# Rotary queries with the dimensions on the partitions, in a decoder layer on one Trainium2 core

## The reference, cut to what matters

```
q = rmsnorm(x @ w_qa, q_norm_w) @ w_qb            # per head: q_nope (128), q_rope (64)
rotate_half(x) = concatenate([-x[..., 32:], x[..., :32]])
q_rope = q_rope * cos + rotate_half(q_rope) * sin
k_rope = k_rope * cos + rotate_half(k_rope) * sin  # one for all heads
scores = (q_nope . k_nope + q_rope . k_rope) / sqrt(192)
```

## Time and profile before

| | |
|---|---|
| median of 3 runs | 1356.03 us (1355.33 to 1356.2) |
| the profiled execution | 1356.68 us, span 1354.9 us |
| busy: PE | 1039.2 us, 77% of the span, 7438 instructions |
| busy: weight loads (PEld) | 632.5 us, 47% |
| busy: DVE | 1088.9 us, 80%, 2984 instructions |
| busy: ACT | 539.4 us, 40% |
| busy: POOL | 239.7 us, 18% |
| mean granted clock of PE | 0.90 |
| chain that ended last | PE 40%, DVE 25%, issue 23%, ACT 5%, POOL 5% |

### The profile page before, as it was taken

How to read it: one execution, slowest core, us unless ns; L and a number is a source line. 1 busy time by engine, 2 the same in 40 slices (tenths; PEclk the granted TensorE clock), 3 DMA queues, 4 the chain that set the end, 5 groups by cost and what they waited for, 6 DMA issues and landing times.

```text
span 1354.9 us, 22533 instructions
## 1 busy us (share of the span) xinstructions
PE 1039.2 (77%) x7438; PEld 632.5 (47%) x7460; DVE 1088.9 (80%) x2984; ACT 539.4 (40%) x1225; POOL 239.7 (18%) x475
## 2 busy tenths in 40 slices
PE   1635687799999999998999999997743552547998
PEld 0423354455555555555555565564332231324554
DVE  5679587988888988988988988887179878876886
ACT  1539444434434434344444444443024321533443
POOL 1000012112112112112112121211022313131111
PEclk9659889999999999999999999999875776767999
DMA  9100022332332342322442333455361000000001
GB/s 360 55 1 0 1 53 49 73 58 57 58 56 54 65 116 53 66 55 46 70 119 47 66 61 61 94 92 147 79 218 39 24 31 0 0 0 8 39 31 47
DMA packets 199388, 86.30 MB, mean 64 GB/s; under 512 B 173560, under 2 KB 184824, under 8 KB 198784
## 3 DMA queue, kind: packets, MB, share of 16 engines
q1 hardware_dynamic: 199296, 85.12, 26.9%
HBM read 35.80 MB, written 7.34 MB: 32 GB/s over the span
## 4 chain that ended last, share of the span: by engine, by line
PE 40%; DVE 25%; issue 23%; ACT 5%; POOL 5%; DMA 1%; ACTq 0%; SPq 0%; DVEq 0%; POOLq 0%
PE bank L1765 10%; PE bank L1715 5%; DVE arena L1438 4%; PE bank L1649 4%; PE bank L1750 4%; DVE arena L1414 3%; PE bank L1681 2%; DVE arena L1431 2%; POOL arena L418 2%; PE bank L1733 2%; PE bank L1737 2%; PE bank L1735 2%; PE bank L1734 2%; PE bank L1736 2%; DVE scal L1532 1%
## 5 line engine op out<-in xcount | busy, mean ns | idle before, releaser
L1160 ACT ACTIVATE arena<-bank,arena,scal 128x128 f32<-128x128 f32 (+3 forms) x256 | 157.9, 617 | 356.6 <-POOL arena L1018 356.6
L1765 PE MATMUL bank<-arena 128*128 128x512 f16 x768 | 187.8, 391 | 7.1 <-DVE arena L1477 4.3
L1438 DVE SCALAR_TENSOR_TENSOR arena<-arena 128x128 f16<-128x128 f32 (+3 forms) x256 | 169.3, 661 | 9.1
L1414 DVE TENSOR_REDUCE arena<-bank 128x1 f32<-128x128 f32 (+3 forms) x256 | 124.2, 485 | 60.4 <-PE bank L1738 60.3
L1018 POOL TENSOR_TENSOR arena<-arena,scal 128x1 f32<-128x1 f32 x256 | 49.0, 191 | 551.2 <-DVE arena L1414 551.2
L1715 PE MATMUL bank<-arena 128*128 128x512 f16 x576 | 136.4, 382 | 0.5 <-DVE arena L1470 0.5
L1750 PE MATMUL bank<-arena 128*128 128x512 f16 (+3 forms) x768 | 116.8, 302 | 10.8 <-DMA arena<-arena 10.8
L1765 PEld LDWEIGHTS bank<-arena 128*128 128x128 f16 x768 | 73.6, 100 | 90.4 <-issue 16.5
L1431 DVE TENSOR_SCALAR arena<-arena 128x128 f16<-128x128 f32 (+3 forms) x256 | 109.9, 429 | 3.0 <-issue 0.3
L1750 PEld LDWEIGHTS bank<-arena 128*128 128x128 f16 x768 | 70.3, 99 | 50.4 <-issue 13.1
L1733 PE MATMUL bank<-arena 128*128 128x128 f16 (+3 forms) x256 | 77.3, 302 | 4.7 <-issue 3.3
(11 more groups left out here) (213 smaller groups left out, 2119.7 us busy)
## 6 DMA issues: line engine op xcount, KB each, us to landing
arena<-in_L_attn_w_qb SPq DMA_DIRECT2D x1, 4608.0 KB, 23.5
arena<-in_x SPq DMA_DIRECT2D x4, 1024.0 KB, 5.9
arena<-in_L_attn_w_o SPq DMA_DIRECT2D x1, 4096.0 KB, 33.9
arena<-arena SPq DMA_TRANSPOSE x256, 2.8
arena<-in_fside_BxS2xS SPq DMA_DIRECT2D x4, 1024.0 KB, 5.7
arena<-in_L_ffn_w SPq DMA_DIRECT2D x8, 512.0 KB, 8.3
out<-arena SPq DMA_DIRECT2D x16, 256.0 KB, 2.0
arena<-in_x SPq DMA_DIRECT2D x12, 256.0 KB, 3.0
```

What stands on the lines that cost most here:

```text
L1160: act.activation(pf(k), banks[S_BANKS[g % 3]][:, 0:n], ACT.Exp, bias=NB[:, k:k + 1], scale=sc_exp, accum_out=SUM[:, k:k + 1]).then_inc(s_e ...
L1414: dve.tensor_reduce(NEGM[:, (g & 3):(g & 3) + 1], banks[S_BANKS[g % 3]][:, 0:n], AX.X, ALU.max, negate=True).then_inc(s_max, 1)
L1438: dve.scalar_tensor_tensor(out=ph_part(k, 1), in0=pf(k).rearrange("p (t c) -> p t c", c=P), scalar=R4[:, k:k + 1], in1=ph_part(k, 0), op0= ...
L1765: last = pe.matmul(banks[Y_BANK][:, :], ot(gp, a, k, (q & 3) * P, P), wo(b, gp * GH + k), start=(k == 0 and n == 0), stop=(k == GH - 1 and ...
```

## The change

The product of the rotary queries is turned round: the weights are the stationary operand and the latents of all 512 tokens the moving one, so the bank holds 128 dimensions (two heads of 64) by 512 tokens after nine instructions. What was a stride within a partition is now a place on another partition. ACT copies the bank to RSW in four pieces of 32 partitions, each to the place of its neighbour (`rope_swap`, at the end of step 3); POOL multiplies RSW by the sine (`rope_sin`); DVE multiplies the bank by the cosine (`rotate`), now behind the splits of step 4, and waits for `rope_swap` before; POOL adds. `rope_hi` stands now in step 6, ahead of `qn_hi_`: one conversion into RHI for the low part and four of 64 partitions into QR, which put each head's rotary part on both halves of the partitions. POOL's `rope_split` writes the low part into QR. The transposes and the copies behind them are gone. The tables are wanted with dimensions on the partitions (COST, SINT): PE transposes them as float32 after the first `prep_mm`, ACT copies them out; the keys keep a table of half the width, for which there is a second load.

```diff
-        ROPE = take(2 * TB * 2 * DR)
+        ROPE = take(2 * TB * DR)
+        COST, SINT = take(L), take(L)
...
-            sp.dma_start(ROPE, rope_tab).then_inc(tab_in, 16)
+            sp.dma_start(ROPE.rearrange("p (a d) -> p a d", d=DR),
+                         rope_tab.rearrange("p (a h d) -> p a h d", h=2, d=DR)[:, :, 0, :]).then_inc(tab_in, 16)
+            sp.dma_start(ROPEF, rope_tab).then_inc(tab_in, 16)
...
+            def rope_sin(i):
+                pool.wait_ge(r_swap, i + 1)
+                pool.tensor_tensor(RSW, RSW, SINT, ALU.mult).then_inc(r_sin, 1)
             def rope_sum(i):
                 pool.wait_ge(r_rot, i + 1)
-                pool.tensor_tensor(RT1, RT1, RT2, ALU.add).then_inc(r_sum, 1)
+                pool.wait_ge(r_sin, i + 1)
+                pool.tensor_tensor(RT1, RT1, RSW, ALU.add).then_inc(r_sum, 1)
+            def rope_split(i, par):
+                pool.wait_ge(r_own, i + 1)
+                pool.tensor_tensor(QR[:, (par * 3 + 2) * L:(par * 3 + 3) * L], RT1, RHI, ALU.subtract).then_inc(r_split, 1)
...
                         if g == 4:
+                            rope_sin(i + 1)
+                        if g == 5:
                             rope_sum(i + 1)
-                        if g == 5:
-                            rope_split(i + 1)
+                        if g == 6:
+                            rope_split(i + 1, 1 - j)
...
+            def rope_swap(i):
+                act.wait_ge(r_mm, i + 1)
+                if i > 0:
+                    act.wait_ge(r_sum, i)
+                for a in range(0, P, 64):
+                    for o in (0, 32):
+                        last = act.activation(RSW[a + o:a + o + 32, :], banks[R_BANK][a + 32 - o:a + 64 - o, :], ACT.Copy)
+                last.then_inc(r_swap, 1)
+            def rope_hi(i, par):
                 act.wait_ge(r_sum, i + 1)
-                act.activation(v[:, :, 1, :], RT1.rearrange("p (a d) -> p a d", d=DR), ACT.Copy)
-                act.activation(v[:, :, 0, :], RT1.rearrange("p (a d) -> p a d", d=DR), ACT.Copy).then_inc(r_hi, 1)
+                act.activation(RHI, RT1, ACT.Copy).then_inc(r_own, 1)
+                for h in range(2):
+                    o = (par * 3 + h) * L
+                    for a in range(0, P, DR):
+                        last = act.activation(QR[a:a + DR, o:o + L], RT1[h * DR:(h + 1) * DR, :], ACT.Copy)
+                last.then_inc(r_hi, 1)
...
                     if g == 6 and not last:
+                        rope_hi(i + 1, 1 - j)
                         qn_hi_(2 * i + 2, 0)
...
-                    if g == 4 and not last:
-                        rope_hi(i + 1)
+                    if g == 3 and not last:
+                        rope_swap(i + 1)
...
             prep_te(0, T_BANK)
+            act.wait_ge(tab_t, 1)
+            act.activation(COST, banks[0][:, :], ACT.Copy).then_inc(tab_made, 1)
+            act.activation(SINT, banks[1][:, :], ACT.Copy).then_inc(tab_made, 1)
...
-                dve.tensor_tensor(RT1, q, c, ALU.mult)
-                dve.tensor_tensor(t4[:, :, 0, :], q4[:, :, 1, :], s4[:, :, 0, :], ALU.mult)
-                dve.tensor_tensor(t4[:, :, 1, :], q4[:, :, 0, :], s4[:, :, 1, :], ALU.mult).then_inc(r_rot, 1)
-            def rope_out_hi(i, par):
-            def rope_out_lo(i, par):
+                dve.wait_ge(r_swap, i + 1)
+                dve.tensor_tensor(RT1, banks[R_BANK][:, :], COST, ALU.mult).then_inc(r_rot, 1)
...
-                for t in range(TB):
-                    k = 0
-                    for c in range(QC):
-                        for a, b in TRI:
-                            last = pe.matmul(banks[R_BANK][:, t * P:(t + 1) * P], ct(bp, a, c, t * P, P),
-                                             wr(b, c, i & 7), start=(k == 0), stop=(k == 3 * QC - 1))
+                for c in range(QC):
+                    for a, b in TRI:
+                        last = pe.matmul(banks[R_BANK][:, :], wr(b, c, i & 7), ct(bp, a, c, 0, L),
+                                         start=(k == 0), stop=(k == 3 * QC - 1))
...
-                    pe.wait_ge(r_teh, i + 1)
-                    pe.wait_ge(r_tel, i + 1)
+                    pe.wait_ge(r_hi, i + 1)
+                    pe.wait_ge(r_split, i + 1)
...
-                        if g == 6:
-                            rope_t_hi(i + 1)
-                        if g == 7:
-                            rope_t_lo(i + 1)
...
             prep_mm(0)
+            rope_tables()
```

More of the change, by code:

```diff
@@ L106, in decoder_layer @@
         XA = take(TB * D)
[L107 removed]
+        RSW = take(L)
+        RHI = take(L, fp16)
         PT = take(2 * 2 * TB * L, fp16)
```

95 lines of the change are left out of this document (32 added, 63 removed).

## The result

| | before | after |
|---|---|---|
| median of six runs, same chip | 1355.8 us | 1349.04 us (1346.42 to 1350.17) |
| profiled execution, and its span | 1356.68, 1354.9 | 1346.42, 1344.6 |
| busy DVE, PE | 1088.9, 1039.2 us | 1043.2, 1016.5 us |
| busy ACT, POOL | 539.4, 239.7 us | 678.7, 273.1 us |

The ratio is 0.9937, 95% interval 0.9915 to 0.9959: 0.6% faster, where 1345.5 us (a ratio of 0.992) was forecast. I read the waits first, as before the change: us in total, times, longest, 160 to 900 us of the changed kernel.

The account below looks back on a forecast made before the run. Neither PE nor DVE is full; they hand the limit to each other through waits. Terms -7 - 5 + 3.8 - 2.3 = -10.5 us on 1356.68 gave 1346.2, median 1345.5; own range 1339 to 1352, wider range 1326 to 1364.

Parts of the forecast that it names:

- pairs 0 to 3: First four head pairs, without output products: little wait of DVE to give, so a gain of 0.
- pairs 4 to 23: Ten double pairs of the walk, each forecast at -0.7 us: together -7 us.
- M7 to M3: From a pair's step 7 row maximum on DVE to the next pair's step 3: 8.85 us odd, 13.2 even.
- M4 to M5: Row maximum of step 4 to that of step 5; in odd pairs from 3.80 to 2.37 us.
- M5 to M7: Row maximum of step 5 to that of step 7; in odd pairs up from 5.57 to 7.2 us, behind ACT's conversions.
- the hold: POOL's sum slowing DVE's 512-column split L1438 before the change, 1.64 for 0.75 us: 0.89 us lost.
- Rival 1: POOL's sine product beats DVE's split in odd pairs and those without preparation: 0.85 us in 20 pairs, 1362 us; chance 0.20.
- The clock: PE's idle time puts preparation products at the lower clock: 1.2 us in one even pair of two.
- +1.5: Ahead of the walk and first pair: tables cost +3.8 us, first pair's rotary chain gains 2.3 us.
- Rival 3: Small ACT copies cost by their partitions, so conversions shrink by 1.1 us in 24 pairs: 1319 us; chance 0.10.
- Rival 4: Walk exchanges PE's wait for ACT's queue and gains nothing: 1357.5 us; chance 0.12.
- Rival 2: Lower clock covers the preparation's products in all 12 even pairs, 2.2 us each, +26: 1371 us; chance 0.08.

Follow-up runs that it names:

- e5: Changed kernel with two full 128x512 conversions instead of four of 64 partitions (rotary scores not the reference's): 1313.56 us, ratio 0.9670.
- e12: Changed kernel with rotary tables built behind the preparation loop and ACT's five conversions split, three after copy L1183, two behind the exponentials: 1316.96 us, ratio 0.9711.
- e4: Changed kernel with the four 32-partition exchange copies replaced by one 128x512 copy, leaving the exchange out: 1356.78 us, ratio 1.0006.
- e14: Kernel with split conversions and late tables, and in even pairs DVE's cosine product put in front of the 128x512 split: 1310.5 us, ratio 0.9669.
- e1: Changed kernel with ACT's five conversions of the rotated queries issued behind the exponential of step 6: 1344.67 us, ratio 0.9920.
- e6: Kernel before the change with DVE's three rotary products moved from in front of the splits to behind them: 1388.84 us, ratio 1.0236.
- e7: Kernel before the change with PE's transposes of the rotated queries' high parts moved from its seventh step to its eighth: 1367.07 us, ratio 1.0070.
- e2: Changed kernel with the rotary tables' eight transposes and two copies moved behind the preparation loop: 1343.0 us, ratio 0.9910.

## Why the prediction was right, and where not

**The sum.** 10.5 us were forecast for the profiled execution and 10.3 measured, and that closeness is partly luck: by sections the start came out 3.5 us better than forecast, pairs 0 to 3 1.7 us and pairs 4 to 23 2.0 us worse. By the medians it is 6.8 us.

**The pairs.** Where the clock was full, every stretch was within 0.11 us of the forecast: odd M7 to M3 8.80 (8.85 forecast; pair 14 to 15), M4 to M5 2.37 (2.37), M5 to M7 7.15 (7.2); even M7 to M3 13.31 (13.2), M3 to M7 15.41 (15.5). The mechanism was the forecast one: PE's wait and the hold go, DVE's wait for L1183 comes. e5 and e12 show that it is this wait which limited the gain. That pairs 4 to 23 gave 5.0 and not 7 lies in the comparison: I took pairs 13 and 14 (51.27) for the mean of before, and ten double pairs take 511.01, 51.10 each. Forecast for after were 50.57, measured 50.6.

**ACT's small instructions.** The price of one was right, the overlap was not: the four start 0.6 us apart, 2.38 and 2.53 us for four, where I took 2.1 and 2.2. Neighbours of 128 partitions had overlapped by 0.1. Half of the 0.6 us falls in M5 to M7, which took the 7.15 us all the same, since from M5 to the first conversion (508.38 to 510.42) it was 2.0 us where I had put 2.3. POOL's sum did fall on the next split, as forecast: L1464 on 128 columns took 0.91 us from 509.56, beside L1035, and 0.29 alone.

**The port.** The sine product did not meet the split in odd pairs. Between L1471's start (507.11) and the exchange's end (507.50) lay 0.4 us, not the 0.2 I had read, and 0.9 from the start of L1464 (506.58). Rival 1 with its price is real (e4), only its condition did not occur. I named the wrong victim: in even pairs it is L1464, with one SBUF operand, and not L1471. The Trainium skill ("SBUF — State Buffer", section "Who interferes with whom") says that a DVE instruction with at most one SBUF input keeps clear of GpSimd only outside the two-port modes, and names `tensor_scalar` among the operations that can use them; the 1.48 us of e4 and the 0.95 of e14 agree.

**The clock.** Forecast: 1.2 us in every second even pair. The penalty was 1.2 us in three of ten (pairs 8, 12, 20), and 0.83 on the way from M7 to M3 of four odd pairs (5, 9, 13, 21), ahead of which products had run slowly behind a wait for a split:

```profile
487.84 4.31 PE L1765 MATMUL bank<-arena 128*128 128x512 f16 x12 [2.42 <-DVE arena L1477]
```

3 x 1.2 + 4 x 0.83 = 6.9 against 6 in the sum: the total was near, half of its places were not. PE's idle time before the preparation's transposes grew as forecast, but to 1.5 to 2.3 us (0.79 before) and not to 2.7.

**Ahead of the walk.** +1.5 was forecast, and this pair of executions reads -2.0. The chain step was near (L1158 at 40.51 against 41.2, +3.1). Then two things gave back: the fourth preparation product ran mostly at the higher clock (granted 0.81 against 0.56), 3.84 us for 5.40, so that the chain was only 1.3 us late at the 8.7-us reduction (80.60 for 79.28), and the rotary product of pair 0, for which I had put 3.8, took 2.10:

```profile
67.56 3.84 PE L1663 MATMUL bank<-arena 128*128 128x384 f16 x24
...
152.26 2.10 PE L1694 MATMUL bank<-arena 128*128 128x512 f16 x9 [1.46 <-DVE arena L1342]
```

Neither belongs to the change. e1 has the same program up to M3 of pair 0; there the fourth product took 5.38 us, and the rotary one

```profile
153.42 3.59 PE L1695 MATMUL bank<-arena 128*128 128x512 f16 x9 [1.46 <-DVE arena L1343]
```

(granted clock 0.57, in the changed kernel's execution 1.00), and M3 of pair 0 came at 177.65, not 174.99. e6 and e7, with the program of before, have it at 175.32 and 177.19 for 177.02. So the clock moves this section by 2 to 3 us from execution to execution, about as much as the forecast and the reading differ by; the -2.0 can't be credited to the change, and whether the +1.5 was right stays open. That the tables cost some 3 us up to the reduction is shown by e2 and the kernels beside it.

**Pairs 0 to 3.** Forecast 0, measured 1.7 lost. I had argued that there is little wait to give there, which was right; but DVE's new wait for L1183 came all the same: M3 to M7 took 12.16 for 11.1 in the odd pairs and 15.43 for 14.7 and 15.0 in the even ones, 3.3 us in four pairs, of which M7 to M3 gave 1.6 back.

**Rivals.** Rival 3 is out (0.587 and 0.624 us). Rival 4 is half true: PE's 32.0 us of waiting became 67.8 us of DVE's, and 5.0 us stayed in pairs 4 to 23. Rival 2 did not come: the lower clock took three of the preparation's products, not twelve.

## What to carry to other kernels

An exchange of partition groups by ACT costs a whole instruction for each group, whatever its height (32 and 64 partitions here); count the instructions. Then place them: the same work cost 27.6 us more or less, as it stood in front of something due or in the idle time between two exponentials. An operation that is moved off PE and DVE is paid where its new engine is next waited for, so ask for each place what queues behind it, and try the split of a long group before any other way round it. Before a saving of 2 or 3 us is read from one execution, look at the same stretch in another kernel with the same program there.

## What the hardware showed that I had not expected

- Four ACT instructions on 32 or 64 partitions in a row don't overlap: 2.38 us for four of 0.587, 2.53 for four of 0.624.
- A copy of 64 KB within SBUF was not cheap for SyncE: 0.6 us to issue one (1.2 for a transposing transfer), 2.1 us from the issue to the landing, so that four took 4.0 us from first issue to last landing (558.21 to 562.20). PE came 0.09 us after the last.
- POOL's product on SBUF operands holds an f32 split by `tensor_scalar` for nearly its whole length (0.49 to 1.47 us; the split ends 0.28 us behind it), and does not slow a product that reads PSUM and SBUF (0.69).
- A wait of 3 us on PE can cost more than itself: the same six products took 2.59 us behind one of 3.13 (granted clock 0.53) and 1.46 behind one of 3.30 (1.00).
